# Expert results by token in DRAM: 4 KB runs, four loads on two queues, finished group by group

## The reference

```python
def _L0_ffn_ref(x, Wr, br, W1, b1, W2, b2):      # x: 2048 tokens x 128, after a layer norm
    logits = xf @ Wr + br                        # 16 experts
    probs = softmax(logits)
    topk_w, topk_idx = top_k(probs, 2)           # two choices for each token
    topk_w = topk_w / maximum(topk_w.sum(-1), 1e-9)
    for e in range(16):
        h = gelu(xf @ W1[e] + b1[e])             # 128 -> 256
        y = y + combine[:, e] * (h @ W2[e] + b2[e])   # 256 -> 128
    return xf + y
h = h + _L0_ffn_ref(_layernorm(h), ...)
```

## Time and profile before

| what | value |
|---|---|
| median of three runs | 230.28 us (230.05 to 231.3) |
| span of the profiled execution | 229.0 us |
| median less span | 1.3 us |
| last scatter issued, landed | 211.16, 213.27 us |
| `parts` loads issued | 213.35 to 217.9 us, eight of them |
| last vector instruction ends | 225.97 us |

### The profile page before, as it was taken

One profiled execution on the slowest core, in us unless ns is written; L12 is line 12 of the kernel. 1 busy time (PEld: TensorE's weight loads), 2 busy tenths in 40 slices (PEclk: granted clock), 3 DMA queues, 4 the chain that ended last, 5 costly groups with the idle time before them and its releaser, 6 DMA issues.

```text
span 229.0 us, 3461 instructions
## 1 busy us (share of the span) xinstructions
PE 163.2 (71%) x833; PEld 111.6 (49%) x833; DVE 122.7 (54%) x511; ACT 94.2 (41%) x256; POOL 100.8 (44%) x158
## 2 busy tenths in 40 slices
PE   4859769886989579608926274899999999991000
PEld 1634434563466266405504131588888888870000
DVE  2531356279587863796562762245555566550174
ACT  2131252525560651145123003467777777760240
POOL 5000520502220672057257472057777777777060
PEclk9999967999799965955785569599999999999555
DMA  1799920000000010001001152234344442100576
GB/s 55 225 340 320 410 88 0 4 0 0 1 3 1 12 59 24 0 12 61 24 24 62 49 177 83 59 89 115 106 119 109 121 112 63 20 17 12 150 217 183
DMA packets 23148, 20.18 MB, mean 88 GB/s; under 512 B 3107, under 2 KB 20813, under 8 KB 22874
## 3 DMA queue, kind: packets, MB, share of 16 engines
q1 hardware_dynamic: 19418, 15.16, 22.5%
q0 software_dynamic: 2560, 4.27, 5.7%
q10 hardware_dynamic: 1152, 0.54, 0.8%
HBM read 13.49 MB, written 7.51 MB: 92 GB/s over the span
## 4 chain that ended last, share of the span: by engine, by line
PE 60%; DVE 14%; ACT 7%; DMA 6%; POOL 6%; issue 5%; SPq 1%; DVEq 0%; POOLq 0%; ACTq 0%
PE bank L979 10%; PE bank L995 9%; PE bank L862 9%; PE bank L986 5%; PE bank L831 4%; DVE stats L597 3%; POOL slots L431 3%; PE bank L934 3%; PE bank L899 3%; PE bank L974 3%; DMA work_b<-parts 2%; PE bank L900 2%; PE bank L902 2%; ACT stage L475 2%; PE bank L842 2%
## 5 line engine op out<-in xcount | busy, mean ns | idle before, releaser
L444 POOL DMA_INDIRECT parts<-work_a,xt x48 | 47.2, 983 | 25.8 <-DVE work_a L770 15.8
L431 POOL DMA_INDIRECT slots<-stage,slot_of x32 | 31.6, 987 | 17.8 <-issue 8.9
L862 PE MATMUL bank<-x1T,convw_sb 128*128 128x512 f32 x48 | 29.2, 756 | 2.5 <-ACT x1T L486 2.5
L979 PE MATMUL bank<-w_sb,xtT 128*128 (+1 forms) x96 | 30.1, 396 | 0.0
L995 PE MATMUL bank<-w_sb,act_hT 128*128 (+1 forms) x192 | 29.8, 278 | 0.0
L764 DVE TENSOR_TENSOR hid<-bank,fb_bc 128x256 f32<-128x256 f32 x48 | 20.4, 425 | 13.3 <-PE bank L979 7.7
L995 PEld LDWEIGHTS bank<-w_sb,act_hT 128*128 128x128 f32 x192 | 25.7, 194 | 0.2 <-ACT act_hT L552 0.2
L770 DVE TENSOR_TENSOR work_a<-bank,fb_bc 128x128 f32<-128x128 f32 x48 | 14.0, 292 | 19.3 <-PE bank L995 19.3
L542 ACT ACTIVATE xtT<-bank 128x128 f32<-128x128 f32 x48 | 13.3, 278 | 20.2 <-PE bank L974 20.2
L420 POOL TENSOR_TENSOR work_c<-work_b,g_bc 128x256 f32<-128x256 f32 x8 | 5.7, 723 | 34.9 <-ACT work_b L475 34.9
L986 PE MATMUL bank<-ident,act_h 128*128 128x128 f32 x96 | 19.4, 284 | 0.3 <-ACT act_h L547 0.3
(11 more groups left out here) (160 smaller groups left out, 272.6 us busy)
## 6 DMA issues: line engine op xcount, KB each, us to landing
xt<-slots SPq DMA_DIRECT2D x48, 66.0 KB, 1.8
w_sb<-in_L_ffn_W_dram SPq DMA_DIRECT2D x1, 2048.0 KB, 9.5
fb_bc<-in_L_ffn_b_dram SPq DMA_DIRECT2D x1, 2048.0 KB, 18.6
fb_bc<-in_L_ffn_b_dram SPq DMA_DIRECT2D x1, 1024.0 KB, 11.2
work_b<-parts SPq DMA_DIRECT2D x4, 256.0 KB, 3.9
work_a<-parts SPq DMA_DIRECT2D x4, 256.0 KB, 5.6
out_dram<-work_c SPq DMA_DIRECT2D x4, 256.0 KB, 2.4
parts<-work_a,xt POOLq DMA_INDIRECT x48, 2.3
```

The lines of the kernel that those rows point to most:

```text
L431: pool.indirect_dma_start(out=slots, out_offset=bass.IndirectOffsetOnAxis(ap=slot_of[:, g, k, s:s + 1].bitcast(U32), axis=0), in_=stage[:, ...
L444: pool.indirect_dma_start(out=parts, out_offset=bass.IndirectOffsetOnAxis(ap=xt[:, u, ROW_PLACE:ROW_PLACE + 1].bitcast(U32), axis=0), in_= ...
L862: last = pe.matmul(by_seq(acc[:]), convw_sb[:, w, half * D:(half + 1) * D], x1T[:, g, :, w:w + L], start=(w == 0), stop=(w == TAPS - 1))
L979: pe.matmul(bank[2 + b][:, 0:HID], xtT[:, b, :], flat(w1_sb[:, expert_of(j), :]), start=True, stop=True).then_inc(t_h_psum, 1)
```

## The change

Row numbers in `parts` become p * 32 + b * 2 + k: all that belongs to one token position lies together, sequence by sequence, with the two choices side by side. A group's share of one position is then 8 rows, 4 KB in a row, and a group is loaded by one DMA of 512 KB that brings both choices. SP loads and stores groups 0 and 2, ACT groups 1 and 3. Groups 0 and 1 land in `work_a`, groups 2 and 3 in `work_b`. DVE works group by group: the fourth block of the next group follows the four final instructions of this one. ACT issues the store of group 1 behind its multiplications for group 2, and that of group 3 at the end.

```diff
+        part_rows = parts.rearrange("(p b k) d -> p b k d", b=SEQS, k=TOPK)
+        halves = GROUPS // 2
+        got = [(work_a, work_b)[g // halves][:].rearrange("p g n -> p (g n)")
+               .rearrange("p (h b k d) -> p h b k d", h=halves, b=GS, k=TOPK)[:, g % halves] for g in range(GROUPS)]
+        token_rows = out.rearrange("b t d -> t b d")
...
+        def load_parts(eng, g):
+            for u in range(U):
+                eng.wait_ge(placed[u], 16 * (TILES // U))
+            eng.dma_start(got[g], part_rows[:, g * GS:(g + 1) * GS]).then_inc(parts_in[g], 16)
+
+        def store_group(eng, g):
+            eng.wait_ge(y_out, g + 1)
+            eng.dma_start(token_rows[:, g * GS:(g + 1) * GS, :], by_seq(work_c[:, g, :])).then_inc(stored, 16)
...
-            for k, buf in ((1, work_b), (0, work_a)):
-                for g in range(GROUPS):
-                    sp.dma_start(by_seq(buf[:, g, :]), both[k, :, g * GS:(g + 1) * GS, :]).then_inc(parts_in[k][g], 16)
...
-            for g in range(GROUPS):
-                sp.wait_ge(y_out, g + 1)
-                sp.dma_start(tokens[:, g * GS:(g + 1) * GS, :],
-                             by_seq(work_c[:, g, :])).then_inc(stored, 16)
+            for g in range(0, GROUPS, 2):
+                load_parts(sp, g)
+            for g in range(0, GROUPS, 2):
+                store_group(sp, g)
...
-                          pattern=[[N, GROUPS], [P, GS], [0, 1]], base=k * T, channel_multiplier=1)
+                          pattern=[[GS * TOPK, GROUPS], [TOPK, GS], [0, 1]], base=k, channel_multiplier=SEQS * TOPK)
...
+            for g in range(1, GROUPS, 2):
+                load_parts(act, g)
             act.wait_ge(base_ready, 1)
             for g in range(GROUPS):
-                act.wait_ge(parts_in[1][g], 16)
+                act.wait_ge(parts_in[g], 16)
                 for s in range(GS - 1):
-                    last = act.activation(blocks(work_c[:, g, :], s), blocks(work_b[:, g, :], s), ACT.Identity,
+                    last = act.activation(blocks(work_c[:, g, :], s), got[g][:, s, 1, :], ACT.Identity,
                                           scale=w_top[:, g * GS + s, 1:2])
                 last.then_inc(scaled_y, 1)
+                if g >= 1 and g % 2 == 0:
+                    store_group(act, g - 1)
+            store_group(act, GROUPS - 1)
...
+            def last_of_group(g):
+                dve.wait_ge(parts_in[g], 16)
+                return mark(dve.scalar_tensor_tensor(
+                    out=blocks(work_d[:, g, :], GS - 1), in0=got[g][:, GS - 1, 1, :],
+                    scalar=w_top[:, g * GS + GS - 1, 1:2], in1=blocks(h0[:, g, :], GS - 1), op0=ALU.mult, op1=ALU.add))
+
+            made = last_of_group(0)
             for g in range(GROUPS):
-                dve.wait_ge(parts_in[0][g], 16)
                 dve.wait_ge(summed, g + 1)
+                dve.wait_ge(dve_chain, made)
...
                 last.then_inc(y_out, 1)
+                if g + 1 < GROUPS:
+                    made = last_of_group(g + 1)
```

More of the change, by code:

```diff
@@ L193, in tower_kernel @@
             sem, ("t_xT_psum", "t_xT", "t_h_psum", "t_h", "t_act", "t_actT_psum", "t_actT", "t_y_psum", "t_y"))
-        parts_in = [[sem(f"parts{k}_in{g}") for g in range(GROUPS)] for k in range(TOPK)]
+        parts_in = [sem(f"parts_in{g}") for g in range(GROUPS)]
         base_ready, stored, scaled_y, summed, y_out = map(sem, ("base_ready", "stored", "scaled_y", "summed", "y_out"))
@@ L352, in _ @@
                 sp.dma_start(xt[:, u, :], slots[bass.ds(row, P), :]).then_inc(xt_in[u], 16)
-            for u in range(U):
-                sp.wait_ge(placed[u], 16 * (TILES // U))
-            both = parts.rearrange("(k b p) d -> k p b d", k=TOPK, p=P)
-            for k, buf in ((1, work_b), (0, work_a)):
-                for g in range(GROUPS):
-                    sp.dma_start(by_seq(buf[:, g, :]), both[k, :, g * GS:(g + 1) * GS, :]).then_inc(parts_in[k][g], 16)
-            tokens = out.rearrange("b t d -> t b d")
-            for g in range(GROUPS):
-                sp.wait_ge(y_out, g + 1)
-                sp.dma_start(tokens[:, g * GS:(g + 1) * GS, :],
-                             by_seq(work_c[:, g, :])).then_inc(stored, 16)
+            for g in range(0, GROUPS, 2):
+                load_parts(sp, g)
+            for g in range(0, GROUPS, 2):
+                store_group(sp, g)
             sp.wait_ge(stored, 16 * GROUPS)
@@ L776, in _ @@
             dve.wait_ge(base_ready, 1)
-            for g in range(GROUPS):
[L778 to L783, removed]
-                dve.wait_ge(parts_in[0][g], 16)
+            def last_of_group(g):
[4 more added lines that the diff above has]
+            made = last_of_group(0)
+            for g in range(GROUPS):
                 dve.wait_ge(summed, g + 1)
+                dve.wait_ge(dve_chain, made)
                 for s in range(GS):
                     last = dve.scalar_tensor_tensor(
-                        out=blocks(work_c[:, g, :], s), in0=blocks(work_a[:, g, :], s), scalar=w_top[:, g * GS + s, 0:1],
+                        out=blocks(work_c[:, g, :], s), in0=got[g][:, s, 0, :], scalar=w_top[:, g * GS + s, 0:1],
                         in1=blocks(work_d[:, g, :], s), op0=ALU.mult, op1=ALU.add)
                 last.then_inc(y_out, 1)
+                if g + 1 < GROUPS:
+                    made = last_of_group(g + 1)
         @block.tensor
```

## The result

The changed kernel takes 235.12 us (median of four runs) against 230.17 for the kernel before on the same chip. The ratio is 1.0197, with a 95% interval from 1.0128 to 1.0266: 4.5 us slower, between 2.9 and 6.1. The forecast was 232.0 in a range up to 233.3. The sign was right and the size was not: +1.75 us were forecast.

What follows compares the result with a forecast made beforehand. DVE alone was taken to set the end. F1's end at 224.0 plus 3.73 put F3's at 227.7; with 3.04 for the last store the span was 230.75, with 1.3 outside it 232.0 us, range 230.0 to 233.3.

Steps and rivals of the forecast that it cites:

- the same 3.04 us to the end: Program end: the last store takes 3.04 us from the end of DVE's work to the span's end, unchanged.
- F3: DVE's four final instructions for group 3, the last vector work; forecast to end at 227.7 us, against 225.97 before.
- The wait of ACT behind the store of group 1: Tail: group 3's multiplications queue on ACT behind that store, which waits for F1; 3.73 us from F1's end to F3's.
- F1: DVE's four final instructions for group 1; forecast to end at 224.0 us, with break-even at 222.24.
- the rival of a hidden wait: Tail: DVE is behind anyway, so the group-3 wait is hidden; gain 0.7 us, total 231.3 us, chance 0.10.
- The stretched instructions, 1.48 us: DVE between F0's start and F1's end: two POOL additions each stretch a DVE instruction by 0.74 us.
- F0: DVE's four final instructions for group 0; forecast to start at 219.95 us, against 220.95 before.
- An even share of two queues: Loads: groups 0 and 1 share the DMA engines evenly and both land at 217.8 us, groups 2 and 3 at 220.35.
- The rival of a landing in order: Loads: group 0 lands before group 1, at 216.5 us; F3 ends at 226.4, total 230.7 us, chance 0.20.
- The rate with 4 KB runs, 410 GB/s: Loads: 4 KB runs move at 410 GB/s, taken between 365 and 426, against 290 for 512-byte runs.
- The scatters and the iotas cost nothing: Before the loads: row numbers cost nothing, scatter landing stays 2.11 us, new addresses allowed 0.3 us either way.
- The 1.3 us outside the span: Measured time beyond the profiled span: kept at 1.3 us, added to a span of 230.75 us.

Runs made afterwards that it cites:

- e1: Changed kernel with ACT's store of group 1 issued behind group 3's multiplications; ratio to the kernel before 1.0040, tail 17.7 us.
- e4: Changed kernel with GpSimd's and ACT's parts of the tail given to DVE; ratio to the kernel before 1.0102, tail 16.7 us.
- e5: Kernel before with DVE doing GpSimd's and ACT's parts of the tail; ratio to the kernel before 0.9951, tail 14.9 us.
- e7: Changed kernel with group 3's second choice done by DVE alone, ACT's store left in place; ratio to the kernel before 1.0080, tail 17.6 us.
- e8: Changed rows and runs, all loads from SP in order, all stores from SP, no GpSimd in the tail; ratio to the kernel before 0.9989, tail 14.6 us.
- e2: Kernel before plus a tiny GpSimd memset behind the last vector instruction; ratio to the kernel before 1.0158, tail 19.1 us.
- e6: Changed kernel with each group's rows side by side in DRAM; ratio to the kernel before 1.0229, tail 20.4 us.
- e3: Changed kernel with all four loads issued from SP; ratio to the kernel before 1.0213, tail 18.8 us.
- e10: e8 measured again unchanged; ratio to the kernel before 0.9948, tail 15.0 us.
- e11: e5 measured again unchanged; ratio to the kernel before 0.9935, tail 15.3 us.

## Why the prediction failed, step by step

- *"From the end of DVE's work, 225.97, to the end of the span are 3.04 us, the last store"*, and after the change "the same 3.04 us to the end". This is the step that failed, and it carries most of the miss: the tail grew by 5.0 us where 1.75 were forecast, and 2.67 of the 3.3 between them are here. What ended the 3.04 was no store but POOL's drain, which happened to lie 0.3 us behind the store's landing. The store alone is 2.7 to 2.8 (e1, e4, e5, e7, e8), so taking it for 3.04 did no harm; that the same 3.04 would stand after the change was wrong. What was queued behind ACT's store was followed to POOL's addition and to F3, but not to POOL's own end. e2 shows the mechanism by itself, e1 and e7 show that it is what the late addition cost, and e6 has the same gap of 5.7 us on a chip where the kernel before takes 247 us, so it was no accident of one execution.
- *The wait of ACT behind the store of group 1.* It is there, and from F1's end to F3's end are 3.80 us (forecast 3.73). But the price in vector work, 0.7 us against the rival of a hidden wait, was wrong: e1 takes the wait away and gains 0.05, since POOL's addition then meets DVE. For the vector work the rival had the right price and not the right reason: DVE was not behind, it did wait 0.88 us for F3.
- *The stretched instructions, 1.48 us.* Right: F0 took 2.59 instead of 1.14, so 1.45, both additions falling into it.
- *An even share of two queues.* Right in the main: groups 0 and 1 landed 4.8 and 5.1 us after their issues, 2 and 3 after 6.6 each. In the records of the DMA engines SP's first 4 KB packet starts at 212.97, ACT's first at 213.49, and from then on both queues are served in turns of a few packets. The rival of a landing in order, and the reading of the packet rule in the Trainium skill (DMA: Bandwidth & Descriptors, "Queues, rings and completion order") by which group 0 would come in whole, did not hold here. That page's other statement, that loads from different engines interleave on the same DMA engines ("Issuing engines are not separate DMA queues"), the trace agrees with.
- *The rate with 4 KB runs, 410 GB/s.* Right at 404. The start was mis-sized: 0.23 us of ramp were taken from before; in the changed kernel 1.3 us ran at 145 GB/s, which loses 1.3 x (1 - 145/404) = 0.83. That is 0.6 us more than the ramp. On the path to F0 0.49 of it shows: F0 started 7.09 us after the first load instead of 6.60. The other 0.12 of the difference between +1.75 and +2.36 are small (F0 to F1 4.09 against 4.04, F1 to F3 3.80 against 3.73). The estimate by the cycles a packet of the Trainium skill (DMA: Bandwidth & Descriptors, "Why small descriptors are slow (HBM only)"), 337 GB/s, was too low.
- *The scatters and the iotas cost nothing.* No run speaks against it: the last scatter landed 2.1 us after its issue, as before, and the 48 scatters start over 60.7 us (before 60.6). One of the prediction's own signs of being wrong did come, an expert stage that ends at another time than 213.3: it ended at 211.9. The shift lies ahead of the scatters into `parts`, as said above.
- *The 1.3 us outside the span.* They were 1.7 to 1.8 in the changed kernel's four executions (234.42 - 232.7 in the profiled one). So 232.0 + 2.7 (the end) + 0.6 (the vector work) + 0.4 (outside the span) - 1.3 (earlier loads) gives 234.4, the time of the profiled execution.

Open is what slows the first packets. One queue instead of two (e3) and rows side by side (e6) leave it. That they are the first reads of rows just written is not enough as a cause: the kernel before reads such rows too, and in the first 1.3 us of its packets their durations beyond the usual 27 ns sum to 0.05 us for each DMA engine, where in the changed kernel those beyond the usual 159 ns sum to 0.7. Whether fresh rows and 4 KB packets together do it was not tried. What the change was worth is now plain too: its loads are in 7.6 us after the first issue, and its finishing by group gives that back by putting POOL's additions among and behind DVE's work. With the same rows, all loads from SP and no POOL (e8, e10) the tail is 5.7 to 6.1 us shorter than in the changed kernel and 0.7 to 1.1 shorter than before. Against the old loads without POOL (e5 and e11, 14.9 and 15.3, where e8 and e10 have 14.6 and 15.0) it is only some 0.3 shorter, less than two profiles of one kernel differ: with POOL out of both tails, no gain of the 4 KB runs is shown. The simplest version, that of e5 and e11, is measured faster than the kernel before in one of two measurements; the tail of the kernel before is itself uncertain by some 0.6 us (in e2, the same up to the memset, the vector work ended at 12.1 and not 12.6), and e11's 0.65% are 1.6 us, where its tail is 0.4 us shorter. Only part of that gain need be the tail.

## What to carry to other kernels

Look at how each engine ends before costing the end of a kernel: here GpSimd needs 6.6 us behind its last instruction (in all thirteen profiles), so its last work must be done that much before the last store has landed, or be given to another engine. An engine that waits behind a store on an in-order queue is to be followed to the program's end, not only to the next consumer. Where GpSimd's help stretches the vector instructions beside it, price the same work on the vector engine too: here twelve more instructions took DVE no longer.

## What the runs showed of the hardware that was not expected

- GpSimd's closing drain ends 6.62 to 6.63 us after its last instruction's end in all thirteen profiles, whether that was a memset of 99 ns, an addition of 1.1 us, or a scatter (e4: last instruction's end at 210.96, drain from 205.74 for 11.83 us, so to 217.57).
- The first 1.1 to 1.3 us of 4 KB loads ran at 145 to 221 GB/s at a DMA share of 0.74 to 0.91, and mostly at 353 to 415 after that (e3 fell to 239 once more).
- The kernel before took 230 us beside the changed kernel and e1 to e4, and 247 on the chips of e5 to e11. The 48 tiles account for most of it: from their first to their last scatter are 60.6 us in the profile of before and 74.9 in that of e5, with the same code there. No run says why.
